# A macaron block of four expert layers and two attentions: first loads in quarters, attention starts and ends rearranged

## The reference

```
x = x + 0.5 * _L0_ffn_ref(_layernorm(x), ...)   # 2 shared + 8 routed gated experts, top 2
x = x + _L0_attn_ref(_layernorm(x), ...)        # 16 heads of 8, band of half width w // 2
x = x + 0.5 * _L0_ffn_ref(_layernorm(x), ...)
x = x + 0.5 * _L1_ffn_ref(_layernorm(x), ...)   # 8 experts, relu squared, capacity
x = x + _L1_attn_ref(_layernorm(x), ...)        # 16 heads of 8, softmax of a hyperbolic distance
x = x + 0.5 * _L1_ffn_ref(_layernorm(x), ...)
```

## Time and profile before

| what | us |
|---|---|
| median of 3 runs | 3094.23 |
| lowest and highest | 3093.03, 3098.08 |
| profiled execution, own time | 3093.71 |
| its span, first to last instruction | 3092.0 |
| P, until the barrier | 0 to about 50 |
| A0 | 419 to 827 |
| A1 | 1600 to 2706 |

### The profile page before, as it was taken

The page is one execution under the profiler, slowest core; times in us unless marked ns, Lnnn a source line. Parts: engine busy times, 40 slices in busy tenths (PEclk is TensorE's granted clock), DMA queues, the critical chain, the costliest instruction groups (busy, mean ns, idle before and its releaser), DMA issues. The chain is left out here.

```text
span 3092.0 us, 42285 instructions
## 1 busy us (share of the span) xinstructions
PE 2596.8 (84%) x12174; PEld 1727.2 (56%) x12208; DVE 2308.9 (75%) x4325; ACT 2207.5 (71%) x2470; POOL 1652.8 (53%) x1312
## 2 busy tenths in 40 slices
PE   5999959999799996999965778777787777579998
PEld 4877845666487784878752223223233332258887
DVE  5677646677467667889968778787787877398887
ACT  3555525566455554777746999999999999667776
POOL 2676652222176664454445576666766767434444
PEclk9999979999899998999986676676766767689999
DMA  3111102222111112111100000000000000021111
GB/s 118 55 41 54 41 11 52 50 48 48 46 49 48 41 54 83 42 55 41 54 0 1 0 1 1 0 1 1 1 1 1 1 1 1 0 111 45 52 47 48
DMA packets 26068, 103.77 MB, mean 34 GB/s; under 512 B 6336, under 2 KB 8384, under 8 KB 16704
## 3 DMA queue, kind: packets, MB, share of 16 engines
q1 hardware_dynamic: 25920, 102.01, 9.7%
HBM read 82.33 MB, written 2.62 MB: 27 GB/s over the span
## 5 line engine op out<-in xcount | busy, mean ns | idle before, releaser
L1792 POOL TENSOR_TENSOR A_Y<-A_Y,A_U 128x2048 f32<-128x2048 f32 x86 | 390.0, 4559 | 226.4 <-ACT A_U L1835 226.4
L1868 DVE TENSOR_SCALAR A_U<-ps 128x1024 f32<-128x1024 f32 x256 | 308.9, 1217 | 127.4 <-POOL A_Y L1792 63.6
L1874 DVE SCALAR_TENSOR_TENSOR A_U<-ps,A_U 128x1024 f32<-128x1024 f32 x256 | 310.8, 1214 | 54.8 <-PE ps L2004 54.8
L2004 PE MATMUL ps<-A_QT,A_KT 9*128 9x512 f32 x512 | 181.6, 706 | 196.8 <-DVE A_U L1874 164.0
L478 POOL TENSOR_TENSOR F0b_h<-F0b_h,dn 128x512 f32<-128x512 f32 x128 | 212.0, 1661 | 112.4 <-DVE F0b_h L410 112.2
L478 POOL TENSOR_TENSOR F0a_h<-F0a_h,dn 128x512 f32<-128x512 f32 x128 | 212.1, 1662 | 104.9 <-DVE F0a_h L410 104.8
L2004 PEld LDWEIGHTS ps<-A_QT,A_KT 9*128 9x128 f32 x512 | 66.0, 254 | 333.1 <-DVE A_U L1874 244.3
L1792 POOL TENSOR_TENSOR dn<-dn,A_U 128x2048 f32<-128x2048 f32 x42 | 190.3, 4553 | 111.8 <-ACT A_U L1835 111.8
L1835 ACT ACTIVATE A_U<-A_U 128x2048 f32<-128x2048 f32 (+1 forms) x96 | 236.5, 2464 | 0.0
L1976 PE MATMUL ps<-A_Y,A_VA 128*32 128x512 f32 x688 | 226.9, 793 | 5.8 <-DVE A_OT L1774 3.0
L1311 DVE CUSTOM_DVE_ANT_0 ps<-ps,A_mask 128x256 f32<-128x256 f32 (+1 forms) x512 | 184.6, 421 | 61.9 <-PE ps L1383 61.0
(11 more groups left out here) (372 smaller groups left out, 8121.5 us busy)
## 6 DMA issues: line engine op xcount, KB each, us to landing
dn<-weight_rows SPq DMA_DIRECT2D x32, 1024.0 KB, 4.6
F1a_cwb<-weight_rows SPq DMA_DIRECT2D x16, 1024.0 KB, 4.6
F1b_cwb<-weight_rows SPq DMA_DIRECT2D x16, 1024.0 KB, 4.7
A_KZ<-A_KT SPq DMA_DIRECT2D x132, 64.0 KB, 2.0
A_QZ<-A_qs SPq DMA_DIRECT2D x96, 64.0 KB, 2.0
dn<-in_down SPq DMA_DIRECT2D x2, 2048.0 KB, 12.3
stage<-in_up SPq DMA_DIRECT2D x1, 2560.0 KB, 8.8
X<-in_x SPq DMA_DIRECT2D x1, 2048.0 KB, 8.4
```

The costliest lines, as they stand in the source:

```text
L1792: eng.tensor_tensor(flat(y_slot(m, h)), flat(y_slot(m, h)), flat(Um[:, h % UR]), ALU.add).then_inc(s["t_ready"], 1)
L1868: eng.tensor_scalar(u_step(n), d_pair(n), 0.0, None, ALU.max).then_inc(s["dp_vector"], 1)
L1874: eng.scalar_tensor_tensor(out=u, in0=g_pair(), scalar=CLAMP, in1=u, op0=ALU.min, op1=ALU.mult).then_inc(s["u_ready"], 1)
L2004: last = eng.matmul(ps[:, 4 + b, :], KT[r:r + 9, pair, kt * P:(kt + 1) * P], QT[r:r + 9, pair, :], start=True, stop=True)
```

## The change

**P**: X comes in four transfers of eight tiles with a semaphore each, and the statistics of chunk c + 1 and the normed tiles of chunk c alternate on VectorE. SyncE then issues the first router, `stage`, `dn0` and three more; ScalarE issues the other 24 small transfers itself, before its first copy. The high part of `stage` is made in four pieces after the copies of chunks 2 to 5; after those of chunks 0, 1, 6 and 7 ScalarE zeroes QA, KA and VA of A0 in eight pieces of 1024. VectorE makes the distances of A0's mask and the low part in four pieces. Semaphores of the weight parts in the expert phases are merged into two, with the same waits.

**A0**: GpSimd zeroes only KZ at the start, and QZ after the first rows. Keys are projected and laid out ahead of queries; the mask's threshold comes after them. Each key transfer carries 24 of a slot's 32 rows. In the loop the wait for these transfers stands behind the wait for the maxima. The last four tiles are turned into banks 0 to 3, without waiting between.

**A1**: for the first chunk ScalarE squares q and k, VectorE makes the columns' reciprocals and assembles the rows, GpSimd only the side columns. Four pieces are turned into banks 4 to 7 ahead of the first scores and twelve within the first burst, two per step for six steps, in banks 6 and 7; ScalarE copies pieces 1 and 3 to 11, VectorE 0, 2 and 12 to 15. At the end the four tiles use banks 0 to 3, VectorE applies the last norm, ScalarE copies its transpose.

The diff's core:

```
@@ phase P @@
-                    eng.dma_start(X[:, :, :], x).then_inc(load["x"], 16)
...
+                    for i in range(PARTS):
+                        tiles = slice(i * TILES // PARTS, (i + 1) * TILES // PARTS)
+                        eng.dma_start(X[:, tiles, :], x[:, tiles, :]).then_inc(x_in[i], 16)
+                    eng.dma_start(rw[0][:, :], router0).then_inc(load["router"], 16)
                     eng.dma_start(stage[:, :], up0).then_inc(load["up0"], 16)
                     eng.dma_start(dn0[:, :, :, :], down0).then_inc(load["rest"], 16)
+                    for dst, src in ((qkv_w[0], w_qkv0), (qkv_w[1], w_qkv1), (out_w[1], wo1)):
+                        eng.dma_start(dst[:, :], src).then_inc(load["small"], 16)
...
+                    for h in range(H):
+                        eng.dma_start(wo_t[h * HD:(h + 1) * HD, h * HD:(h + 1) * HD], wo0_t[h]).then_inc(load["small"], 16)
+                    cleared = [(qa, 0), (qa, 1024), (ka, 0), (ka, 1024), (qa, 2048), (qa, 3072), (va, 0), (va, 1024)]
                     for c in range(B):
                         eng.wait_ge(s["tr_done"], c + 1)
                         eng.activation(XT[:, c * S:(c + 1) * S], ps[:, c % 6, :], ACT.Copy).then_inc(s["xt_copied"], 1)
+                        if 2 <= c < 2 + PARTS:
+                            if c == 2:
+                                eng.wait_ge(load["up0"], 16)
+                            cols = slice((c - 2) * part, (c - 1) * part)
+                            eng.activation(up0_hi[:, :, :].rearrange("p u n -> p (u n)")[:, cols], stage[:, cols],
+                                           ACT.Copy).then_inc(s["split_done"], 1)
+                        else:
+                            for n in range(2 * (c % 4), 2 * (c % 4) + 2):
+                                flat, lo = cleared[n]
+                                eng.activation(flat[:, lo:lo + 1024], zero[:, :].to_broadcast([P, 1024]), ACT.Copy)
...
+                    stats(0)
                     for c in range(B):
+                        if c + 1 < B:
+                            stats(c + 1)
                         eng.wait_ge(s["rstd_ready"], c + 1)
...
+                    eng.tensor_scalar(A0_mask[:, :], dist[:, 1, :], 2.0, None, ALU.mult)
@@ first attention, start, GpSimd; transfers; VectorE; PE @@
-                        for a in (KZ, QZ):
-                            eng.memset(a[:, :, :, :].rearrange("p n j q -> p (n j q)").bitcast(F32), 0.0)
+                        eng.memset(KZ[:, :, :, :].rearrange("p n j q -> p (n j q)").bitcast(F32), 0.0)
                         eng.drain().then_inc(pad_ready, 1)
...
                         eng.wait_ge(s["qs_ready"], 1)
+                        rows_k(0)
+                        eng.wait_ge(s["qs_ready"], 2)
                         rows_q(0, 0)
-                        eng.wait_ge(s["qs_ready"], 2)
-                        rows_k(0)
+                        eng.memset(QZ[:, :, :, :].rearrange("p n j q -> p (n j q)").bitcast(F32), 0.0)
+                        eng.drain().then_inc(pad_ready, 1)
...
-                                eng.dma_start(KZ[r:r + 32, g % 2, j, :].bitcast(F32),
-                                              KT[r:r + 32, g, :].bitcast(F32)).then_inc(s["kz_ready"], 16)
+                                eng.dma_start(KZ[r:r + 3 * HD, g % 2, j, :].bitcast(F32),
+                                              KT[r:r + 3 * HD, g, :].bitcast(F32)).then_inc(s["kz_ready"], 16)
...
+                        take_k(0)
                         take_q(0)
-                        take_k(0)
+                        mask_of_columns()
...
+                                if t == 0 and i == 0:
+                                    eng.wait_ge(s["kz_ready"], spreads(TPC * c + g + 1))
...
+                        project(1)
+                        eng.wait_ge(s["qs_ready"], 1)
                         project(0)
-                        eng.wait_ge(s["qs_ready"], 1)
-                        project(1)
-                        eng.wait_ge(step, n0 + 5)
+                        eng.wait_ge(s["asm_done"], 1)
+                        turn(0, KA, 0)
                         eng.wait_ge(s["asm_done"], 2)
-                        turn(0, KA, 0)
@@ first attention's end, PE (the second's is the same) and VectorE @@
                         for t in range(TPC):
-                            turn_out(eng, B, t)
+                            for g in range(4):
+                                last = eng.transpose(ps[:, t, g * P:(g + 1) * P], OT[:, g, t * P:(t + 1) * P], ident[:, :])
+                            last.then_inc(s["on_tr"], 1)
...
+                            eng.wait_ge(s["on_tr"], TPC * B + t + 1)
+                            v = ps[:, t, :].rearrange("p (h r) -> p h r", r=32)
+                            eng.reciprocal(rden_4[:, t, :], v[:, :, HD])
+                            eng.drain()
+                            eng.tensor_tensor(on[:, t, :].rearrange("p (h d) -> p h d", d=HD), v[:, :, 0:HD],
+                                              rden_4[:, t, :].unsqueeze(2).to_broadcast([P, H, HD]),
+                                              ALU.mult).then_inc(s["on_ready"], 1)
@@ second attention's start, ScalarE and GpSimd @@
+                def first_squares_scalar(eng):
+                    eng.wait_ge(s["k_done"], 1)
+                    eng.activation(oT[:, :], ps[:, 7, :], ACT.Square).then_inc(s["s_ready"], 1)
+                    eng.wait_ge(s["q_taken"], 1)
+                    eng.activation(sq[:, :], ps[:, 6, :], ACT.Square).then_inc(s["s_ready"], 1)
...
+                def first_bank(i):
+                    return 4 + i if i < 4 else 6 + i % 2
...
+                            if first:
+                                first_squares_scalar(eng)
+                                for i in (1, 3):
+                                    turned_scalar(eng, i, first_bank(i))
+                                for i in range(4, 12):
+                                    turned_scalar(eng, i, first_bank(i))
...
-                        sides_gpsimd(eng, 0)
-                        assemble_gpsimd(eng, 0)
+                        first_sides_gpsimd(eng)
...
+                                if first and i < 6:
+                                    for n in (4 + 2 * i, 5 + 2 * i):
+                                        eng.wait_ge(s["turned"], n - 1)
+                                        turn_tensor(eng, 0, n, first_bank(n))
@@ second attention's end @@
-                        apply_norm_gpsimd(eng, B, B - 1)
-                        keep_norm_gpsimd(eng, B, B - 1)
+                        norm_gpsimd(eng, s, B)
...
+                        norm_stats_vector(eng, s, B, B - 1)
+                        norm_apply_vector(eng, s, B, B - 1)
+                        norm_logits_vector(eng, s, B, B - 1, nxt, 0)
```

More of the change, by code:

```diff
@@ L729, in macaron @@
             iota_i = sb("iota_i", [P, E], I32, st)
+            zero = sb("zero", [P, 1], F32, st)
+            dist_i = sb("dist_i", [P, WIN], I32, st)
+            dist = sb("dist", [P, 2, WIN], F32, st)
+            PARTS = 4
+            x_in = [sem(f"x_in{i}") for i in range(PARTS)]
             def body(block):
@@ L789, in _ @@
                         if c == 1:
-                            eng.wait_ge(load["small"], 16 * (12 + H))
+                            eng.wait_ge(load["router"], 16)
                         if c > 0:
@@ L797, in _ @@
                     last.then_inc(s["lg_done"], 1)
+                    eng.wait_ge(load["small"], 16 * (11 + H))
                     eng.matmul(ps[:, 6, 0:D], wo_t[:, :], wfc[:, :], start=True, stop=True).then_inc(step, 1)
@@ L816, in _, with stats @@
                 def _(eng):
-                    eng.wait_ge(load["x"], 16)
-                    for c in range(B):
+                    def stats(c):
+                        if c % (B // PARTS) == 0:
+                            eng.wait_ge(x_in[c * PARTS // B], 16)
                         tiles = range(TPC * c, TPC * (c + 1))
@@ L993, in attn0 @@
                     s, lay, lambda t, g: OT[:, g, t * P:(t + 1) * P], on, oT, rden[:, :], SPARE)
[L994 to L996 removed]
+                mask = A0_mask
                 mask_b = ab("mask_b", [P, 2 * WIN], BF16)
@@ L1120, in chunk @@
                                 spread_keys(turned + 3 * g, (g + 1) % 4)
+                                if not done and g == 1:
+                                    eng.wait_ge(pad_ready, 2)
                                 if done or g > 0:
@@ L1390, in shifted @@
                             n = UNITS * c + u
+                            if isinstance(n, int) and n == 0:
+                                eng.wait_ge(step, n0 + 5)
                             lo, hi, w0, w1 = window(m)
@@ L1884, in burst @@
                                     after(i)
-                            for i in range(4):
-                                turned_vector(eng, c, EARLY + i, WINDOW_BANKS[i])
```

(21 more changed lines are left out.)

262 lines of the change are left out of this document (163 added, 99 removed).

## The result

| | before | after |
|---|---|---|
| median (runs) | 3095.33 us (4) | 3041.76 us (4) |
| lowest to highest | 3093.03 to 3098.08 | 3040.69 to 3044.65 |
| ratio, 95% interval | | 0.9828 (0.9811 to 0.9845) |
| span of the profiled execution | 3092.0 | 3040.1 |

The account below looks back on a forecast made before the run. It took the attentions' middles to be full (PE in the first, ScalarE in the second), leaving gains at five edges: 17.0 + 13.7 + 2.9 + 11.3 + 5.2 = 50.1 us off 3093.7, giving 3043.6, range 3034 to 3055.

Parts of the forecast that it names:

- P: First phase, before the first attention: quartered X and overlapped weight parts save 17.0 us (13 to 19).
- The rival of dear issues by ScalarE: First phase: ScalarE's issues at 1.0 us each, so 6.5 gained there, not 17; 3054 us; chance 0.07.
- that of transfers in series: First phase: each transfer pays its fixed time in turn; sum 43.2 less, kernel 3050.5 us; chance 0.03.
- A0's start: Start of the first attention: fewer fills and keys ahead of queries bring the first score 13.7 us earlier (12.5 to 14.5).
- A0's end: End of the first attention: four banks let the last tiles pass without PE waiting, 2.9 us less (2.0 to 4.5).
- A1's end: End of the second attention: four banks 2.9, norm on VectorE 2.2, copy on ScalarE 0.1; 5.2 us less (4.5 to 6.5).
- What follows is as before: End of the first attention: the steps behind the four tiles' rounds keep their times, so they add no gain.
- the upper bound: First attention's end, 4.5 us less: PE starts turning back at full clock; should it last, two later steps gain too.
- A1's start: Start of the second attention: earlier rows and only four turns before the first scores save 11.3 us (9 to 14).
- That the shift would pass on through ScalarE: Second attention: ScalarE idle until its first large root, the bound after, so the earlier start's 11.3 us reach the end.
- The 24 rows and the order of the waits: First attention: smaller key transfers cost 0; moving their wait costs nothing found, or 2.6 us if first weight loads show.
- The case of more than forecast: Whole kernel: first quarter of X at 3.2 us and the clock held at both ends give 3033 us; chance 0.03.

## Why the prediction was right, and where it was off

**What bounds the kernel.** Right: the middles did not move (1031.1 and 1031.3; 358.3 and 359.0), the edges did, and each edge's gain passed its barrier (the expert phases behind them gave back nothing, -0.9 in all).

**P: 17.0 forecast, 16.0 measured.** The chain held link by link (first use 5.2 forecast, 6.2 measured; last normed tile 25.7 and 26.9; `stage` at 17 and 17.2). What was mis-sized is the first quarter: issued at 0.82 and used at 6.21, it took 5.4 us where I had 3.1 + 1.3 = 4.4. What I had left out is the other transfers beside it: with `stage` 10 us later and the small ones one behind the other, as in the run with the small transfers by SyncE, the quarter took 4.0. By the fit of the Trainium skill ("DMA: Bandwidth & Descriptors", "Anatomy of one DMA — SWDGE (gpsimd) path"), which is for another kind of issue, the quarter would take an estimated 3.2 us; neither time bears that out. The rival of dear issues by ScalarE fell (0.36 and 0.63 each), that of transfers in series too.

**A0's start: 13.7 and 13.25.** The keys were turned 10.4 us after the start, 10.8 forecast. Two undone parts gave 3.2 (order; forecast 3.1) and 7.1 (fills; forecast 7.0). What I put at 0, the 24 rows, cost 0.65 here.

**A0's end: 2.9 and 4.5; A1's end: 5.2 and 7.3.** This is the step that failed. "What follows is as before" is wrong: the clock of the steps behind the rounds gave 1.4 more in each, which I had only in the upper bound, and A1's 7.3 is beyond its bound of 6.5. The rows for it were there: of the same size, the first transposes took 0.63 and the turning back behind the pauses 1.12. The run with one bank shows that it hangs on the pauses, and the granted clock (0.50 with them, 1.00 without, in the turning back) that it is the clock. The rounds themselves gave 3.2 in each where I had 2.9, since VectorE's part took 0.53 per tile, not 0.64.

**A1's start: 11.3 and 10.8.** I had 12.5, less 1.2 for VectorE's short instructions beside GpSimd's columns. The sums came 0.4 earlier than forecast, but from them to the first turning it took 5.3 us instead of 4.3, so the first turning was 0.5 later. Of the last two subtractions the one that began before GpSimd's copy took 0.38, the one that began after it 0.77. So the 1.2 stood against 1.0 at most. Laid end to end, as I priced the rule of the Trainium skill ("SBUF — State Buffer", "Who interferes with whom") for all of GpSimd's columns, it would have been 3.3, and it was not; whether the shared port is the reason for the 0.77 was not isolated. From the first turning to the first maximum it took 0.2 more than forecast. The burst took 23.2 us, where I had 21.6 + 0.6: PE's turnings and scores alternate in its first 8 us at 1.2 GHz (granted clock 0.50) and VectorE once waits 1.25 us for a difference. 0.5 + 0.2 + 1.0 is what the 10.8 lacks to 12.5. That the shift would pass on through ScalarE was right.

**The 24 rows and the order of the waits.** Forecast 0. The rows cost 0.65 at the first score, and nothing that can be told apart in the loop. The order of the waits was tried only together with them.

**The sum.** 50.1 forecast, 51.9 by the spans, 53.6 by the medians. The ends' clock (+2.8), their rounds (+0.6) and A1's last steps (+0.4) stood against P (-1.0), the two starts (-1.0), A0's loop (-0.7) and A1's middle (-0.2); the expert phases added 0.9, by chance as far as their 1 us differences in other profiles tell. That the sum came within 1.8 is partly luck: misses of 4.7 on one side met 2.9 on the other. The case of more than forecast, 3033, holds half of what happened, the clock at both ends, but does not add up: the quarter at 3.2 (1.0) and both ends at their upper bounds (1.6 and 1.3) give 3039.7. A1's norm on VectorE (2.2 forecast and measured) was not undone by itself, nor were the merged semaphores.

## What to carry to other kernels

Where the middle of a phase is full, read its two edges for what is serial: a transfer that could be used in parts, a producer that does the second thing first, tiles that take turns in one buffer though others are free. Cost each edge link by link; P and the two starts came out within 1 us here, the ends 1.6 and 2.1 off. Where a first transfer is on the path, count what goes out beside it: here that cost 1.4. And where PE pauses often for under a microsecond, price the instructions behind the pauses at both of their durations in the trace, and read the granted clock beside them: removing the pauses changed the next two steps here, and the later ones, behind another gap, stayed slow.

## What the runs showed of the hardware

- Of sets of four transfers, those of 24 rows x 512 took longer to issue than those of 32 rows: 3.21 us for the first set of keys in the changed kernel, 2.50 with 32 rows, 2.51 before. Over all 132 key transfers the median issue took 0.71 us with 24 rows and 0.59 with 32. From the last issue's end to the score that waits it was 1.5 and 1.6 us, so the landing does not differ. The Trainium skill ("DMA: Bandwidth & Descriptors", "Why a DMA increments its semaphore by 16 and not by 1") gives 24 rows to 12 of the engines and 32 to 16, two rows each either way, and lets the issuing engine write the count that is missing to 16. By that the load of each engine is the same; whether the extra write is what costs the time, no run here shows.
- A transfer took longer with more issued beside it: X's first quarter 5.4 us with `stage` issued 2.5 us behind it and small transfers by ScalarE from the start, 4.0 with `stage` 12 us behind it and the small ones by SyncE; X undivided 9.0 (`stage` 0.9 us behind it) and 8.4 (12.4 us).
- A set of 36 idle transposes did not keep PE's clock up over a gap of 4.6 us; 26 and 22 of them kept it over gaps of 1.9 and 2.3 us in the ends, though in A1's end it was back at 0.50 for the step after.
- The first burst of A1 took 23.2 us where the granted clock was 1.00 from 8 to 14 us into it, 24.5 where it was 0.50 there, with the same instructions, and 23.6 once where the 1.00 lay earlier.
- An edit in the first phase lengthened the middle of A1 by 4 us in both of its profiles (1035.9, against 1029.4 to 1032.3 in eleven profiles of the others); the cause is open.
